# Swin attention block on one core: three of an image's four transposes of the row maxima are issued ahead of the values of an odd step

## The reference

```
y = roll(layernorm(x, g1, b1), (-2, -2))          # cut into 8*16 windows of 128 tokens
q, k, v = split(y @ qkv_w + qkv_b)                # q scaled by 8 ** -0.5
attn = softmax(q @ k.T + bias[rel_pos] + mask)    # 128 x 128 a head and window
o = roll((attn @ v) @ proj_w + proj_b, (2, 2))
x = x + o
return x + gelu(layernorm(x, g2, b2) @ fc1_w + fc1_b) @ fc2_w + fc2_b
```

## Time and profile before

| | |
|---|---|
| median of three runs | 229.96 us |
| the profiled execution, first to last instruction | 228.1 us |
| TensorE matmul busy | 210.0 us, 92% |
| VectorE busy | 165.0 us, 72% |
| ScalarE busy | 148.7 us, 65% |
| GpSimd busy | 128.1 us, 56% |
| mean granted TensorE clock | 0.993 |

### The profile page before, as it was taken

One profiled execution on the slowest core, in us unless ns is written; L12 is line 12 of the kernel. 1 busy time (PEld: TensorE's weight loads), 2 busy tenths in 40 slices (PEclk: granted clock), 3 DMA queues, 4 the chain that ended last, 5 costly groups with the idle time before them and its releaser, 6 DMA issues.

```text
span 228.1 us, 8128 instructions
## 1 busy us (share of the span) xinstructions
PE 210.0 (92%) x3352; PEld 119.5 (52%) x3352; DVE 165.0 (72%) x253; ACT 148.7 (65%) x217; POOL 128.1 (56%) x116
## 2 busy tenths in 40 slices
PE   0899877999999999999999999999999999979884
PEld 0755432655566556655665566566556555443221
DVE  3896757557777787878797876786766757866874
ACT  7475356757676677677757675867546555577883
POOL 8765688272457956784788397632742092150740
PEclk9999998899999999999999999999999999999999
DMA  6825356545424532552364045305530000000233
GB/s 193 250 73 177 108 165 188 175 152 180 131 91 138 167 93 93 158 154 76 104 179 142 10 139 160 123 14 165 166 98 1 6 6 4 4 0 3 106 124 138
DMA packets 24284, 25.41 MB, mean 111 GB/s; under 512 B 3556, under 2 KB 21732, under 8 KB 24164
## 3 DMA queue, kind: packets, MB, share of 16 engines
q1 hardware_dynamic: 23496, 24.16, 34.0%
q10 hardware_dynamic: 752, 0.74, 1.2%
HBM read 16.24 MB, written 8.39 MB: 108 GB/s over the span
## 4 chain that ended last, share of the span: by engine, by line
issue 40%; POOL 36%; PE 10%; ACT 6%; DVE 3%; DMA 2%; SPq 1%; POOLq 1%; ACTq 0%; DVEq 0%
POOL rstd L376 17%; POOL X L406 4%; POOL parts L394 4%; POOL yn L386 3%; POOL X L411 3%; POOL xc L368 3%; PE ps L962 3%; DMA slots<-parts 2%; ACT q_rows L740 1%; POOL mean L356 1%; ACT k_rows L740 1%; POOL var L362 1%; PE pq L962 1%; PE pav L992 1%; PE ps L1014 1%
## 5 line engine op out<-in xcount | busy, mean ns | idle before, releaser
L524 DVE TENSOR_REDUCE negm<-ps 128x8 f32<-128x1024 f32 x64 | 78.1, 1223 | 32.8 <-PE ps L898 32.7
L735 ACT ACTIVATE prob<-ps 128x1024 f32<-128x1024 f32 x64 | 65.5, 1023 | 40.1 <-PE ps L925 40.0
L376 POOL TENSOR_TENSOR rstd<-var,neghalf 128x16 f32<-128x16 f32 x16 | 47.4, 2963 | 17.1 <-DVE var L489 16.2
L912 PE MATMUL ps<-rel_j,id_b 96*32 96x512 bf16 x512 | 39.9, 385 | 3.1 <-ACT prob L735 2.2
L945 PE MATMUL pav<-prob,va 128*32 128x128 f32 x1024 | 41.5, 280 | 0.0
L945 PEld LDWEIGHTS pav<-prob,va 128*32 128x32 f32 x1024 | 24.2, 109 | 12.6 <-issue 5.2
L876 PE MATMUL ps<-rel_i,ident_b 64*64 64x512 bf16 x256 | 26.5, 404 | 0.2 <-DVE negm L524 0.2
L925 PE MATMUL ps<-q_rows,k_rows 64*128 64x128 bf16 x512 | 25.6, 220 | 0.0
L394 POOL TENSOR_TENSOR parts<-rest,parts 128x512 bf16<-128x512 f32 x15 | 17.3, 1157 | 13.8 <-ACT parts L719 13.8
L898 PE MATMUL ps<-k_rows,q_rows 64*128 64x128 bf16 x512 | 25.0, 218 | 0.0
L925 PEld LDWEIGHTS ps<-q_rows,k_rows 64*128 64x128 bf16 x512 | 14.5, 95 | 15.2 <-issue 15.1
(11 more groups left out here) (134 smaller groups left out, 336.2 us busy)
## 6 DMA issues: line engine op xcount, KB each, us to landing
slots<-parts SPq DMA_DIRECT2D x21, 256.0 KB, 2.3
q_rows<-slots SPq DMA_DIRECT2D x42, 128.0 KB
k_rows<-slots SPq DMA_DIRECT2D x40, 128.0 KB
X<-x_tok SPq DMA_DIRECT2D x8, 256.0 KB, 3.9
y_tok<-res SPq DMA_DIRECT2D x7, 256.0 KB, 2.0
q_rows<-m_hi SPq DMA_DIRECT2D x32, 4.0 KB
q_rows<-m_mid SPq DMA_DIRECT2D x32, 4.0 KB
bias_parts<-rel_parts SPq DMA_DIRECT2D x3, 128.0 KB
```

The source lines that it names most:

```text
L376: pool.tensor_tensor(rstd[:, i, :], var[:, i, :], neghalf[:], ALU.pow).then_inc(rstd_done[i], 1)
L524: dve.tensor_reduce(dst, first_home(j)[:].rearrange("p (a u n) -> p a u n", u=2, n=TOK), AX.X, ALU.max, negate=True).then_inc(max_done, 1)
L735: act.activation(prob[:, j % NPROB, :], ps2[:], ACT.Exp).then_inc(exp_done, 1)
L912: pe.matmul(ps2[32 * c:32 * (c + 1), 512 * e:512 * (e + 1)], id3_b[0:96, :], rel_j[0:96, c, e].unsqueeze(2).to_broadcast([96, 2, 2, TOK]), ...
```

## The change

The groups get a table of their own, `max_group(p)`: group p/2 + 1 stays in the even step p with s=0 (and in p = -2); group (p + 1)/2 goes to the odd steps s=3, s=5 and s=7. In the steps s=2, 4 and 6 nothing of the maxima is left. ScalarE, VectorE and SyncE ask the same table. On TensorE the transposes of the odd steps stand ahead of the values.

```diff
+        def max_group(p):
+            if p == FIRST + 2:
+                return 0
+            if p < 0 or p % PPI not in (0, 3, 5, 7):
+                return None
+            k = p // 2 + 1 if p % PPI == 0 else (p + 1) // 2
+            return k if k < GROUPS else None
...
         @block.sync
-                if p % 2 == 0 and 0 <= (p + 2) // 2 < GROUPS:
-                    send_max((p + 2) // 2)
+                if max_group(p) is not None:
+                    send_max(max_group(p))
...
         @block.vector
-                if p % 2 == 0 and 0 <= (p + 2) // 2 < GROUPS:
-                    middle_max((p + 2) // 2)
+                if max_group(p) is not None:
+                    middle_max(max_group(p))
...
         @block.scalar
-                if p % 2 == 0 and 0 <= (p + 2) // 2 < GROUPS:
-                    high_max((p + 2) // 2)
+                if max_group(p) is not None:
+                    high_max(max_group(p))
...
         @block.tensor
                     project_v(b + 1)
+                if p % 2 == 1 and max_group(p) is not None:
+                    transpose_max(max_group(p))
...
                     weighted_values(p - AV_LAG)
                 if 0 <= p < PAIRS:
                     bias_s2(p)
-                if p % 2 == 0 and 0 <= (p + 2) // 2 < GROUPS:
-                    transpose_max((p + 2) // 2)
+                if p % PPI == 0 or p == -2:
+                    transpose_max(max_group(p))
```

## The result

The change is slower by about 2%. Beside the first runs of the kernel before the ratio was 1.023 [1.018, 1.029], 235.31 us against 230.15; in a second series 1.019 [1.016, 1.022], 234.39 against 230.1. The forecast was 227.2, with a range up to 230.4. The profiled execution spans 234.0 us, 5.9 more than before.

What follows compares the result with a forecast made beforehand. The prediction took TensorE as the bound, with the exponential as last wait at the ends of s=2 and s=6. TensorE's gain of 3.4 us less 0.6 for sends gave 2.8, so 227.2 us, range 225.8 to 230.4.

Steps and rivals of the forecast that it cites:

- the one on SyncE: SyncE, s=5 to next s=0: group 4's send arrives just as needed; 0.1 us charged at six boundaries, 0.6 us.
- Rival A: At s=0, sends arrive late through SyncE's full queue: wait 0.9 x 6 = 5.3 us, 231.9 us; chance 0.2.
- the sum: SyncE's issue times from s=5 plus landing: group 4's m_mid lands at 119.6, needed at 119.62.
- the landing: Group 4's m_mid send to the second scores of s=0: landed 1.3 us after its issue.
- The loose bound of 2.18: Loosest landing bound in the trace, m_mid's issue to its reader's start: 2.18 us, 0.9 us per boundary.
- The LOW scatter: In SyncE's queue ahead of group 4's send: the LOW scatter takes 0.46 us.
- The argument against rival A: In SyncE's order, group 5's send also stands right behind four gathers, and its reader waits for nothing.
- the other sends: Group 2 issued by about 106.5, needed at 108.4; group 3 by 112.4, needed at 114.0: they have room.
- TensorE's own terms: On TensorE: 4.7 us gone between biases, 0.9 added in s=5, 0.4 in the slow-clock stretch: 3.4 us gained.
- rival B: On TensorE, the moved transpose is as dear in its new place, 0.205 per neighbour: 228.7 us; chance 0.15.
- the regular image of 21.5 us: A regular image, 21.95 us before the change, should take 21.5.
- rival C: In the shortened steps VectorE or ScalarE becomes the last wait, eating the gain: 229.7 us; chance 0.1.

Runs made afterwards that it cites:

- e9_low_scatter: The changed kernel with only the LOW scatter moved behind the send of group 4, to s=7: 231.27 us, ratio 1.005.
- e4_sync_edges: The changed kernel with MID scatter and HIGH q_rows gathers one step earlier, first and last moved groups back between the biases: 234.77 us, ratio 1.021.
- e7_best: The changed kernel with HIGH k_rows gathers behind group 4's send, MID gathers behind s=0's send, first and last moved groups put back: 226.19 us, ratio 0.985.
- e5_send_first: The changed kernel with the three HIGH gathers of k_rows behind the send of group 4 instead of ahead of it: 228.97 us, ratio 0.997.
- e8_before_sync: The kernel before, no transpose moved, with HIGH gathers of k_rows and MID gathers each later by one send: 229.66 us, ratio 1.000.
- e2_s7_only: The kernel before with only group 4 moved, from s=6 to s=7: 230.33 us, ratio 1.002.
- after_again: The changed kernel run once more beside the kernel before on the same chip: 234.39 us, ratio 1.019.

## Why the prediction was wrong

The step that failed is the one on SyncE. It had the send of group 4 arrive just as it is needed and charged 0.1 us at each of six boundaries; measured were 0.9 to 1.4, 6.9 us instead of 0.6. Rival A had the right mechanism, and its price, 0.9 x 6, was even too small. I gave it 0.2.

In the sum the m_mid of group 4 was issued 5.95 us behind that of group 3; in the six images it was 6.5 to 6.9. And the landing, 1.3 in the sum, was 1.7 to 1.9 up to the reader's start. The two terms, for the image shown:

- *The landing.* I took the end of the packets' burst, 1.3 us behind the issue, as the moment from which TensorE can read. The same view of the changed kernel, 40 slices of 0.07 us from 121.2, shows m_mid's burst end with the 21st slice, by 122.7, so again 1.3 behind 121.35, but the reader starts at 123.21, 1.86 behind the issue.

```profile
GB/s 146 161 219 205 249 234 264 190 249 293 322 278 176 103 29 15 0 0 0 33 26 0 0 0 0 0 0 0 0 0 73 190 263 278 307 278 220 132 73 59
```

  Over the eight waits of the changed kernel it is 1.6 to 1.9. Here that is +0.56. The loose bound of 2.18 was above all eight, as the 1.3 was below them. The Trainium skill ("DMA: Bandwidth & Descriptors", Anatomy of one DMA), whose 2.0 us include the completion, was the better guide, though it gives them for GpSimd's path: they would have put the reader 0.14 later than the trace has it.
- *The LOW scatter.* I took 0.46 from a place where two small sends stood ahead of it; directly behind three gathers it took 1.04 with its gap (117.86 to 118.90), +0.58. In the six images it was 0.63 to 1.17. Besides, in four of the six a run of three gathers took 2.20 to 2.39 and not 1.86. The sum used the 1.86 although had a run of 2.58. e9_low_scatter shows that time which leaves this queue comes off the wait, and also that only half of the scatter's time left it.

The rest of the queue's sum held in the image shown: the m_hi of group 3 was issued 7.95 us ahead of the moment of need, where 7.8 was forecast, and the two gather runs took 1.86 and 1.82. (The sum itself has a slip: its terms give 117.79 and not 117.75 for m_hi of group 4. It changes nothing.)

The argument against rival A was no test of it. Today's send of group 5 stands behind seven gathers and its reader waits for nothing, but that send has 4.2 us from its issue to its reader, where the moved send of group 4 had 0.9 left from its issue to the moment of need:

```profile
121.41 0.54 SPq L262 DMA_DIRECT2D q_rows<-m_mid  x1
```

```profile
125.64 0.40 PE L925 MATMUL ps<-q_rows,k_rows 64*128 64x128 bf16 x8
```

*The ends.* I gave the other sends room, by the regular image alone, and put them at nothing. The last group's send (moved from step 60 to 61) was not worked out: m_mid is issued at 203.31 and read at 204.93, a wait of 1.0, which is gone in e4_sync_edges and e7_best. In the first image TensorE waits 1.0 in step 4; that wait is in e7_best as well and is not shown to come from the change.

```profile
203.35 0.61 PE L920 MATMUL ps<-rel_j,id_b 96*32 96x512 bf16 x8
204.93 0.40 PE L933 MATMUL ps<-q_rows,k_rows 64*128 64x128 bf16 x8 [0.96 <-DMA q_rows<-m_mid]
```

*What held.* TensorE's own terms: 0.205 gone in each shortened step of the regular images; 0.11 added in s=5 and not 0.21 (rival B is out: from the two L1060s to the values it is 0.48, 117.17 to 117.65, where it was 0.36 before, from the L1052 at 104.25 to the values); nothing added in s=3 and s=7, where the exponential is still the last wait; the regular image of 21.5 us, which e7_best has with 21.44 and the changed kernel, with its wait, with 22.43; and the time of e7_best, 226.19, where the same sum gave 226.4. VectorE and ScalarE did not become the bound (rival C): the steps are shorter by the full 0.205, and the row maxima and exponentials still wait for TensorE.

So the change does save TensorE the 3 to 4 us that were forecast, and SyncE's order takes them and 4 to 6 us more.

## What to carry to other kernels

When an operation is moved, work out the whole way of its result to its reader, through each queue it joins, in the fullest stretch and in the first and last steps, before counting what its old place gains; a path that ends at zero has no room when one of its terms is known only to lie between 1.3 and 2.2 us. Evidence that a late place in the queue does no harm counts only from a send that had as little time. Size a DMA from its issue to its reader's start where the reader waits, not to its last packet. A small send that a matmul waits for goes ahead of bulk gathers in a DMA queue: here one such exchange was worth 5 to 6 us (e5_send_first), and a like order nothing in a kernel in which the sends had time (e8_before_sync).

## What was not expected of the hardware

- The reader of a 4 KB DMA started 1.6 to 1.9 us behind its issue in the eight waits of the changed kernel. In steps 62 and 32 the last packet came 1.3 us behind the issue in both, and the reader 0.3 and 0.5 behind that. The shortest was 1.62, in step 62, with no gathers about.
- A scatter directly behind three gathers held its issuer for 0.5 to 1.1 us instead of 0.37 (1.59 once in e2_s7_only), and three gathers took 1.8 to 3.5 us in the same place of different images (e2_s7_only). Where the scatter was taken away, gathers took up about half of its time (e9_low_scatter).
- The transpose of 16 columns added 0.11 to 0.12 us among 128x128 operations and 0.21 between bf16 ones of 64 x 64 and 96 x 32.
- Behind an idle time of 1.30 in step 48 and one of 0.32 at the start of step 49 the granted clock fell from the level of 2.4 GHz to that of 1.2 (0.50 from 170.3 to 173.0 us) and cost 1.5 us. In the profile of after_again, with 1.00 in step 48 and 0.32 in step 49, it did not fall there.
